# Node stages of a graph network as pipelines over quads of tiles, and edge passes in units of 128 slots

## The reference

```python
def _mlp(h, W1, b1, W2, b2, g, beta):
    h = silu(h @ W1 + b1)
    h = silu(h @ W2 + b2)
    mu = mean(h, axis=-1, keepdims=True)
    var = mean(square(h - mu), axis=-1, keepdims=True)
    return g * (h - mu) * rsqrt(var + LN_EPS) + beta

# layer 1, on h = relu(layernorm(x))
edge_attr = _mlp(edge_attr_3, emb_...)              # 50000 x 128
for l in range(2):
    msg_in = concatenate([h[dst], h[src], edge_attr], axis=1)
    edges_new = _mlp(msg_in, e...[l]) + edge_attr
    agg = segment_sum(edges_new, dst, N)
    h = _mlp(concatenate([h, agg], axis=1), n...[l]) + h
    edge_attr = edges_new
x = x + h
# input of layer 2
h = relu(layernorm(x))
hidden = h @ L2_W.T + b                              # then gathered by edge
```

## Time and profile before

| | us |
|---|---|
| median of three runs | 4950.51 |
| the profiled execution | 4946.26 |
| its span, first to last instruction | 4944.4 |

### The profile page before, as it was taken

One profiled execution on the slowest core, in us unless ns is written; L12 is line 12 of the kernel. 1 busy time (PEld: TensorE's weight loads), 2 busy tenths in 40 slices (PEclk: granted clock), 3 DMA queues, 4 the chain that ended last, 5 costly groups with the idle time before them and its releaser, 6 DMA issues. The chain is left out here.

```text
span 4944.4 us, 75576 instructions
## 1 busy us (share of the span) xinstructions
PE 3421.8 (69%) x18153; PEld 2337.9 (47%) x18154; DVE 2516.8 (51%) x8840; ACT 1365.9 (28%) x3054; POOL 2183.6 (44%) x2148
## 2 busy tenths in 40 slices
PE   2488883665899999159999748888655555465553
PEld 1366662112566666037777526666443333233332
DVE  6655664776555543557776355655533222432222
ACT  0177771661111100025555314555320000000000
POOL 0577884000000000037777007777305777447774
PEclk7587885787999999569999659999855555565555
DMA  1222222000000000246667225454401111232223
GB/s 52 39 63 63 65 63 84 0 0 10 18 16 17 16 14 16 72 121 181 181 185 171 49 64 137 129 128 128 65 1 53 53 53 53 59 130 53 53 53 60
DMA packets 265942, 342.35 MB, mean 69 GB/s; under 512 B 82123, under 2 KB 174805, under 8 KB 264077
## 3 DMA queue, kind: packets, MB, share of 16 engines
q1 hardware_dynamic: 195810, 218.28, 14.3%
q0 software_dynamic: 69856, 120.70, 12.7%
HBM read 240.63 MB, written 97.70 MB: 68 GB/s over the span
## 5 line engine op out<-in xcount | busy, mean ns | idle before, releaser
L2005 PE MATMUL gat_acc<-gat_rows,gat_hot 128*128 128x128 f32 x1664 | 578.5, 479 | 484.5 <-issue 246.4
L907 PE MATMUL hop_p_a<-hop_h,adj 128*128 128x384 bf16 x4375 | 724.8, 328 | 29.3 <-DVE hop_h L848 29.3
L2005 PEld LDWEIGHTS gat_acc<-gat_rows,gat_hot 128*128 128x128 f32 x1664 | 401.3, 316 | 663.0 <-issue 662.2
L1663 POOL DMA_INDIRECT lb_far<-far_rows,lb_idx x440 | 432.0, 982 | 361.7 <-DVE lb_idx L1768 227.9
L907 PEld LDWEIGHTS hop_p_a<-hop_h,adj 128*128 (+1 forms) x4375 | 429.3, 98 | 317.8 <-DVE hop_h L848 36.9
L1663 POOL DMA_INDIRECT la_far<-far_rows,la_idx x440 | 425.7, 968 | 302.0 <-DVE la_idx L1768 168.2
L1989 POOL DMA_INDIRECT gat_rows<-hidden_rows,gat_idx x416 | 396.3, 953 | 352.1 <-DVE gat_idx L2012 225.6
L1394 POOL DMA_INDIRECT by_src_records<-scatter_rec,scatter_rank x384 | 481.0, 1253 | 129.4 <-issue 115.7
L1989 POOL DMA_INDIRECT gat_rows<-typed_rows,gat_idx x416 | 394.8, 949 | 230.7 <-DVE gat_idx L2012 104.2
L2020 DVE TENSOR_SCALAR gat_hot<-iota_row,gat_tabs 128x128 f32<-128x128 f32 x416 | 148.2, 366 | 370.9 <-PE gat_acc L2005 365.0
L519 POOL DMA_INDIRECT tabby_src_by_src_tab_rec<-by_src_records,by_src_off x4 | 4.0, 1000 | 735.2 <-ACTq L594 734.3
(11 more groups left out here) (509 smaller groups left out, 6672.9 us busy)
## 6 DMA issues: line engine op xcount, KB each, us to landing
edge_features<-emb_out SPq DMA_DIRECT2D x110, 256.0 KB
la_feat<-edge_features SPq DMA_DIRECT2D x110, 256.0 KB, 3.2
edge_features<-la_out SPq DMA_DIRECT2D x110, 256.0 KB
lb_feat<-edge_features SPq DMA_DIRECT2D x110, 256.0 KB
la_place<-dst_row SPq DMA_DIRECT2D x110, 128.0 KB
lb_place<-dst_row SPq DMA_DIRECT2D x110, 128.0 KB, 3.3
typed_rows<-typed_np_row SPq DMA_DIRECT2D x25, 512.0 KB, 2.6
hop_side<-x0share_nodes SPq DMA_DIRECT2D x125, 64.0 KB
```

Of the source, the lines that this page charges most:

```text
L907: ins = nc.tensor.matmul(p_a[(u.par + r) % 2][:, 0:3 * D], K.adj[:, s, bass.ds(u.t * P, P)], h3[r % 2][:, s, :, :].rearrange("p i d -> p ( ...
L1663: pool.indirect_dma_start(out=far[g % FAR][:, k, :], out_offset=None, in_=dr.far[:, :], in_offset=bass.IndirectOffsetOnAxis(ap=idx[:, g * ...
L2005: nc.tensor.matmul(acc[:, bass.ds(at[u % LOADS], D)], hot[u % HOTS][:, :], rows[u % RING][:, :], start=False, stop=True, skip_group_check= ...
```

## The change

The unit is 128 slots instead of 256: a group has UG = 4 units, there are 416 units in GE = 104 groups (403 of them hold edges, so three groups hold none), each group has twelve near products of 128 columns instead of six of 256, four additions to `K.sum` instead of two, and the register load reads sixteen numbers instead of eight. `aggregate` is gone: the share beta * degree is added by DVE within the loop of the edge pass (`beta_share`, for seven quads of tiles), and g * sum and the addition to `K.agg` move to the node stage.

`node_update` works on quads of four tiles (the seventh has one). Each engine runs rounds; in round r TensorE has the transposes of quad r, the second product of quad r-1, the transposes of the new rows of an older quad, the first product of quad r and the last product of the older quad. Statistics and roots are made per quad. GpSimd makes g * sum, the addition to `K.agg` and the residual base (h + beta, and + x in layer 1) with `tensor_tensor` on 128 x 512. In layer 1 the stage goes on to x, its layernorm with relu and the rows `hidden`; `conv_input` is gone. Stores are one or two DMAs per quad.

```diff
-UE = 256
+UE = 128
+UG = GS // UE
...
-        tile_row[0:1, 2 * g:2 * (g + BATCH)], engines=[engine], min_val=0, max_val=(NT - 1) * P,
+        tile_row[0:1, UG * g:UG * (g + BATCH)], engines=[engine], min_val=0, max_val=(NT - 1) * P,
...
                 for k in range(4):
-                    j = k // 2
-                    ins = nc.tensor.matmul(p_s[g % 2][:, j * D:(j + 1) * D], hot[g % 3][:, k, :], n[g % 3][:, k, :],
-                                           start=(k % 2 == 0), stop=(k % 2 == 1))
+                    ins = nc.tensor.matmul(p_s[g % 2][:, k * D:(k + 1) * D], hot[g % 3][:, k, :], n[g % 3][:, k, :],
+                                           start=True, stop=True)
...
-                for j in range(2):
+                for j in range(UG):
                     if g > 0 or j > 0:
-                        dve.wait_ge(s_add, 2 * g + j)
-                    total = sums[:, :, :].rearrange("p t d -> p (t d)")[:, bass.ds(at[g % BATCH * 2 + j], D)]
+                        dve.wait_ge(s_add, UG * g + j)
+                    total = sums[:, :, :].rearrange("p t d -> p (t d)")[:, bass.ds(at[g % BATCH * UG + j], D)]
                     nc.vector.tensor_tensor(total, p_s[g % 2][:, j * D:(j + 1) * D], total, ALU.add).then_inc(s_add, 1)
...
-                for j in range(2):
+                for j in range(UG):
                     cols = slice(j * UE, (j + 1) * UE)
                     for i in range(3):
-                        nc.tensor.matmul(p_z[g % 2][:, cols], near[:, i, bass.ds(at[g % BATCH * 2 + j], D)],
+                        nc.tensor.matmul(p_z[g % 2][:, cols], near[:, i, bass.ds(at[g % BATCH * UG + j], D)],
                                          spread[g % 2][:, cols], start=False, stop=False)
...
+            def beta_share(q):
+
+                c = min(4, NT - 4 * q)
+                ch(nc.vector.tensor_tensor(share[:, 0:c, :], beta_row[:, :].unsqueeze(1).to_broadcast([P, c, D]),
+                                           K.deg[:, 0, 4 * q:4 * q + c].unsqueeze(2).to_broadcast([P, c, D]), ALU.mult))
+                ch(nc.vector.tensor_tensor(K.agg[:, 4 * q:4 * q + c, :], K.agg[:, 4 * q:4 * q + c, :], share[:, 0:c, :],
+                                           ALU.add))
...
             for g in range(END):
+                if 8 <= g < 8 + 4 * NB and g % 4 == 0:
+                    beta_share((g - 8) // 4)
...
-            aggregate(nc, ch, K, g_row, beta_row)
...
+QUADS = [list(range(4 * q, min(4 * q + 4, NT))) for q in range((NT + 3) // 4)]
...
+    cols = D if last else 2 * D
+    TURN, PROD = (3, 4) if last else (2, 3)
...
+        @block.gpsimd
+        def _(pool):
+            cp = Chain(pool, s_pc)
+            pool.wait_ge(s_ge, 16)
+            for q in range(Q):
+                if q > 0:
+                    cp(nc.gpsimd.tensor_tensor(nodes(K.sum, q), nodes(K.sum, q), wide(ge_row, q), ALU.mult))
+                    cp(nc.gpsimd.tensor_tensor(nodes(K.agg, q), nodes(K.agg, q), nodes(K.sum, q), ALU.add))
+                    pool.sem_inc(s_agg, 1)
+                else:
+                    pool.wait_ge(s_w, LOADS * 16)
+                    pool.wait_ge(s_agg, 1)
+                ins = nc.gpsimd.tensor_tensor(nodes(K.sum, q), nodes(K.h, q), wide(beta_row, q), ALU.add)
+                if last:
+                    cp(ins)
+                    ins = nc.gpsimd.tensor_tensor(nodes(K.sum, q), nodes(K.sum, q), nodes(K.x, q), ALU.add)
+                ins.then_inc(s_base, 1)
...
+            for r in range(Q + PROD):
+                if live(r):
+                    turned(r)
+                if r == 0:
+                    pe.wait_ge(s_w, LOADS * 16)
...
+                if live(r - 1):
+                    second(r - 1)
+                if live(r - TURN):
+                    turned_new(r - TURN)
+                if live(r):
+                    first(r)
...
+                if live(r - TURN):
+                    product(r - TURN)
...
+            for r in range(Q + PROD):
+                if not last and live(r - PROD):
+                    high(r - PROD)
+                    middle(r - PROD)
+                if live(r):
+                    evict(r)
+                if live(r - 1):
+                    rows(r - 1)
+                if live(r - TURN):
+                    new_T(r - TURN)
+                if live(r):
+                    hidden(r)
+                if live(r - 1):
+                    norm(r - 1, r)
+                if last and live(r - 2):
+                    next_norm(r - 2, r)
...
+            for r in range(Q + PROD):
+                if live(r - PROD):
+                    if last:
+                        biased(r - PROD)
+                    else:
+                        split(r - PROD)
+                        low(r - PROD)
+                if live(r - 1) or (last and live(r - 2)):
+                    roots(r)
+                if live(r - 1):
+                    update(r - 1)
...
-def conv_input(nc, A, K, dr):
...
-        conv_input(nc, A, K, dr)
```

397 lines of the change are left out of this document (255 added, 142 removed).

## The result

The changed kernel takes 4713.93 us (median of four runs, 4712.35 to 4716.08), the kernel before 4951.45 in the same comparison: a ratio of 0.9521, 95% interval 0.9504 to 0.9537. Predicted were 4718 us, 4685 to 4762. The profiled execution has a span of 4714.3 us, 230.1 less than before.

A forecast was written before the change was run, and what follows sets the result against it. POOL's gather issue bounds the edge passes, engine chains the node stages; layout 1.5, embedding -4, edge passes -43 and -48, node stages -63 and -76 sum to -232.5: 4713.8 from 4946.3, 4718 us on the median's footing, range 4685 to 4762.

The forecast's parts named there:

- The edge passes: Both pass loops: 104 groups instead of 110 at POOL's gather pace, aggregate gone (-16 each); -43 in pass 0, -48 in pass 1.
- the 8 us set aside for TensorE and VectorE: Pass 0 loop: +5 for TensorE's twelve near products and +3 for DVE's extra additions and beta_share.
- VectorE's sum: Pass 0: DVE's 3.92 us per group plus two more additions, given as 4.67, under the 5.1 pace; +3 taken.
- The embedding pass: Embedding loop: six groups fewer, -28; additions and register load, +22; 2 us at the end; sum -4, bounds -22 to +8.
- The layout: Tables before the embedding pass: four pieces instead of two, two indirect loads and small operations more; +1.5 us (0 to 3).
- The node stages: Layer 0: 97 us against 160.3, -63. Layer 1 with the convolution's input: 93 against 169.1, -76.
- So TensorE, at half clock, is the pace: Node stages: TensorE's work at clock 0.50 sets the rounds, 13.1 us per quad in layer 0, 11.1 in layer 1.
- the ring from silu over statistics and roots, normalisation and update: Node stage rounds: chain from silu over roots to the new rows, about 10 us, counted as below TensorE's 13.1.
- all hidden: Node stages: GpSimd operations at 1.5 us each add no cost; rival of dear ones, 4.4 us each, +45, chance 0.08.
- start and fill: Node stages, before the rounds: layer 0 start 7 and pipe fill 3 us; layer 1 start 7.5 and fill 3.
- TensorE as the pace of pass 0: Rival, edge pass 0: TensorE instead of POOL's gathers sets the period; +10 to +20, about 4735 us; chance 0.12.
- The slower case: Rival, edge passes: narrow products cost a fixed 0.2 us or more each; at 0.32, +530, about 5245 us; chance 0.02.

## Why the prediction was right, and where it was not

*The edge passes* were right by their steps: fewer groups, `aggregate` off the path, GpSimd's issue still the pace. Pass 0 gave -42.0 where -43 was forecast, pass 1 -47.9 where -48. In most groups of pass 0 the twelve near products took 0.67 us, as their columns have it and as I took them. The part that I had not seen is the slow groups: their mean of 0.78 us in pass 0 and 1.00 in pass 1 adds 0.1 and 0.35 us per group, which was hidden under the gathers' 5.1, in pass 1 with more room. That pass 0 comes within 1 us is luck in part: the 8 us set aside for TensorE and VectorE were taken up by a period of 5.16 instead of 5.10 us, and that is GpSimd's gather at 0.986 instead of 0.968 us, a term that the sum did not have. The seven kernels with units of 128 that ran at the usual pace have 0.978 to 0.986 us there, the three with 256 have 0.967 or 0.968; why is open. VectorE's sum has a slip, 3.92 + 0.70 is 4.62 and not 4.67, which changes nothing; but its additions are waited for in pass 0 (5.9 of 400 us), as the +3 allowed.

*The embedding pass* came out +4.1 instead of -4. The mechanism was the one forecast, additions and register load in the chain that TensorE waits for, and its terms were mis-sized: per batch +0.85 for the additions where I had 0.63, +0.50 for the load where I had 0.2, the upper end of my bounds being 0.65. 26 x 1.35 = 35 against 28 saved is +7, and the loop grew by 6.8. That this meets so closely is luck too: the old loop took 506.4, 507.9 and 518.7 us in three kernels with the same code in it. What I had not seen is that this chain was worth far more than its own length, 35 us: with it out of the way the loop falls by 92 us, 57 of them waits of TensorE and 36 its own time at a higher clock. Which of the two brings the other about is not shown. I priced a loop at a fixed 4.64 us per group which was in truth a mixture of 17.1, 19.1 and 20.5 us batches.

*The layout* gave -3.4, not +1.5. All kernels with units of 128 started the embedding pass at 188.6 to 193.3 us, the three with 256 at 194.5 to 195.1. Which step of the layout it is I did not look for.

*The node stages* were near in size (92.5 for 97, 98.4 for 93) by a step that failed: "So TensorE, at half clock, is the pace". TensorE waits in every round, its clock is 0.72 and 0.68, eight transposes more per quad change nothing, and six operations fewer on VectorE shorten the stages by 8 and 10 us. The pace is the ring from silu over statistics and roots, normalisation and update, which I had named ("about 10") and set aside; it is 9.7 us in a full round. From the first normalisation to the last the six rounds take 54.6 us against the 78.6 of 6 x 13.1, 24 us less, and some 19 of them are lost again at the start: *GpSimd* is not dear, 1.26 us an operation, but not "all hidden" either. The prediction put nothing in the sum for what its work does to VectorE, and gave start and fill 10 us; the first normalisation comes 29.7 us into the stage, 18.3 with GpSimd idle. Two errors of opposite sign made a good number. In layer 1 they no longer cancelled: the forecast's round was shorter there, 11.1 us, while the measured one is 9.6, as in layer 0. So the rounds gave back 11 us only and the tail 5, the first normalisation came at 32.5 us instead of 10.5, and the stage was 5 us longer than forecast.

The rivals: TensorE as the pace of pass 0 came within 0.2 us per group, its waits in the rows above. The slower case fell by the 65 and 83 ns that a narrow product takes on average in the two passes, against 0.20 us needed.

## What to carry to other kernels

When a stage becomes a pipeline, write out the ring of dependences of a round beside the sum of each engine, and take the longer; the engine that was busiest before is often not the one that sets the round. Work moved to GpSimd is not free for VectorE even if nothing waits for it: in stages like these, price each GpSimd operation as time in which VectorE's short casts and arithmetic stand. In a loop where VectorE serves another engine, put what is waited for at the top of the iteration, and split a loop into batches with their clock before taking its mean as a constant.

## What the runs showed of the hardware that was not expected

- VectorE's casts, `tensor_scalar` and two-input operations that meet a running GpSimd `tensor_tensor` of 128 x 512 end only with it: they take up to 1.4 us instead of 0.16 to 0.28. Its statistics do not: four BN_STATS take 0.88 us and four BN_AGGR 0.38 with and without it. Twenty-one such GpSimd operations on a tile of their own made two stages 13.3 and 14.3 us longer. The Trainium skill, "GPSIMD Engine Reference", section "Specifications", names contention on shared SBUF interfaces with VectorE instructions in a 2-port perf mode or with two SBUF inputs. The rows of two-input operations agree with it; for the cast, with one input, the first of the two conditions would have to hold, and no row says in which mode an instruction ran.
- Twelve bf16 products of 128 columns at a register's column start 56 ns apart in most groups of pass 0, 0.67 us for all, and 119 to 131 ns apart in parts of others, up to 1.3 us for all; what distinguishes these is not shown.
- The register load in VectorE's stream lasts 0.60 us for eight numbers and 1.10 for sixteen. Behind a long operation a part of it is covered: with the additions ahead of the roots VectorE stands 0.77 us there instead of 1.15.
- The same batch of the same code took 17.1 us at a granted clock of 0.90 and 20.5 at 0.75, and the share of each kind changed a loop by 12 us between two kernels with equal code in it.
- Indirect DMAs of edge passes ran at 5.1 to 5.2 us per four in most sessions and at 6.5 to 6.7 in two, for every kernel profiled there; the kernel before took 430 and 570 us longer in these two. Each of the later sessions ran on a chip of its own, so whether it is the chip or the time is not told apart.
